# A message-passing kernel on one core: both edge tiles of a slot split into an fp32r pair, six block numbers in a word, three routing columns on GpSimd

## The reference, cut to what matters

```python
def _L0_gnn_ref(h, e, d2, ...):          # h = layernorm(x), d2 = edge weight
    hi, hj = h[e[0]], h[e[1]]
    msg = silu(concatenate((hi, hj, d2), -1) @ mW1 + mb1)
    msg = layer_norm(msg, ln_g, ln_b)
    msg = silu(msg @ mW2 + mb2)
    agg = segment_sum(msg, e[0], num_segments=3125)
    y = silu(concatenate((h, agg), -1) @ uW1 + ub1) @ uW2 + ub2
    return h + y
x = x + _L0_gnn_ref(layernorm(x), stack([src, dst]), edge_weight1, ...)
x = x + ffn(layernorm(x))   # top half of the nodes by a score goes through a gelu MLP
```

## Time and profile before

| | us |
|---|---|
| median of 3 runs | 2267.47 (2264.85 to 2274.99) |
| the profiled execution, whole | 2273.0 |
| its span | 2271.0 |
| TensorE busy | 1969.9 (87%) |
| VectorE busy | 1733.3 (76%) |
| ScalarE busy | 1314.6 (58%) |
| GpSimd busy | 1237.7 (54%) |

### The profile page before, as it was taken

How to read it: one execution, slowest core, us unless ns; L and a number is a source line. 1 busy time by engine, 2 the same in 40 slices (tenths; PEclk the granted TensorE clock), 3 DMA queues, 4 the chain that set the end, 5 groups by cost and what they waited for, 6 DMA issues and landing times. The chain is left out here.

```text
span 2271.0 us, 45335 instructions
## 1 busy us (share of the span) xinstructions
PE 1969.9 (87%) x11037; PEld 1679.3 (74%) x11038; DVE 1733.3 (76%) x4528; ACT 1314.6 (58%) x2595; POOL 1237.7 (54%) x1178
## 2 busy tenths in 40 slices
PE   3546674379999999999999999999999999799996
PEld 1324553267888888888888888888888888677775
DVE  5789999667778778778777787787787787436795
ACT  2322331256667777777776776777777677433331
POOL 7753222466666666666666666666666666503000
PEclk9987776589999999999999999999999999999998
DMA  3000000343333333333333333333333333010001
GB/s 123 0 1 21 26 26 18 102 136 124 87 87 95 92 87 93 97 87 94 96 93 86 94 96 87 91 95 93 90 94 95 88 92 92 1 40 2 27 1 57
DMA packets 107787, 165.05 MB, mean 73 GB/s; under 512 B 42141, under 2 KB 78330, under 8 KB 107485
## 3 DMA queue, kind: packets, MB, share of 16 engines
q0 software_dynamic: 42016, 111.40, 18.0%
q1 hardware_dynamic: 59822, 47.94, 6.8%
q10 hardware_dynamic: 5900, 5.08, 0.7%
HBM read 152.30 MB, written 11.65 MB: 72 GB/s over the span
## 5 line engine op out<-in xcount | busy, mean ns | idle before, releaser
L917 POOL DMA_INDIRECT g_rows<-b_table,idx_ring x792 | 763.3, 964 | 485.1 <-ACT act L967 277.8
L1048 PE MATMUL ps<-w2g,nT 128*128 128x256 f32 x3336 | 789.1, 379 | 0.0
L1048 PEld LDWEIGHTS ps<-w2g,nT 128*128 128x128 f32 x3336 | 601.5, 190 | 64.5
L956 ACT ACTIVATE normed<-act,shift,rstd_e 128x255 f32<-128x255 f32 x834 | 450.1, 590 | 16.1 <-DVE shift L1115 13.7
L1031 PE MATMUL psG<-msg,ohf 128*125 128x256 f32 x1668 | 429.9, 380 | 0.4 <-issue 0.4
L972 ACT ACTIVATE nT<-psM 128x512 f32<-128x512 f32 x417 | 248.7, 596 | 309.9 <-PE psM L1040 234.3
L1082 DVE TENSOR_TENSOR agg<-psG,agg 125x256 f32 x834 | 348.9, 418 | 88.2 <-PE psG L1031 30.9
L1022 PE MATMUL psH<-a_sb,ohT 128*128 x1668 | 348.1, 332 | 40.2 <-DVE ohT L1135 35.5
L1146 DVE TENSOR_TENSOR g_rows<-psH,g_rows 128x512 f32<-128x512 f32 x417 | 285.4, 684 | 67.2 <-issue 27.5
L1152 DVE BATCH_NORM_STATS2 stat_e<-act 128x6 f32<-128x256 f32 x834 | 311.0, 415 | 14.6 <-ACT act L967 14.6
L1022 PEld LDWEIGHTS psH<-a_sb,ohT 128*128 128x128 f32 x1668 | 260.1, 192 | 68.7 <-issue 48.4
(11 more groups left out here) (196 smaller groups left out, 1995.8 us busy)
## 6 DMA issues: line engine op xcount, KB each, us to landing
loc_rows<-loc_d SPq DMA_DIRECT2D x139, 187.5 KB
g_rows<-b_table,idx_ring POOLq DMA_INDIRECT x792
h_sb<-in_x SPq DMA_DIRECT2D x1, 3125.0 KB
b_table<-b_out SPq DMA_DIRECT2D x25, 125.0 KB
x_all<-in_x ACTq DMA_DIRECT2D x1, 3125.0 KB
out<-x_all SPq DMA_DIRECT2D x5, 625.0 KB
ohT<-ew_d SPq DMA_DIRECT2D x139, 9.0 KB
idx_ring<-rec SPq DMA_DIRECT2D x132, 3.0 KB
```

The costliest lines, as they stand in the source:

```text
L917: pool.indirect_dma_start(g_rows[:, j, n, :], None, b_table[:, :], bass.IndirectOffsetOnAxis(ap=which, axis=0)).then_inc(s_gather[j], 16)
L956: ins = nc.scalar.activation(normed[:, j % 2, n, 0:D - 1], act1[:, (j - 10) % RING, n, 0:D - 1], ACT.Identity, scale=rstd_e[:, g % 2, k:k ...
L1048: mm = pe.matmul(ps2[:, k, n, :], nT[:, k, n, q, :], w2g[:, q, :], start=(q == 0), stop=(q == 1))
```

## The change

- Each block's list is padded to a multiple of 256 edges, so both tiles of a pair belong to one block. PAIRS becomes 429, TILES 858.
- ScalarE writes the SiLU of ps twice: to high, rounded to fp32r, and, after act1, in full into ps2 (PSUM), over its input. VectorE makes low = ps2 - high (fp32r) as the last thing in its slot. TensorE sums ohf x high and ohf x low of both tiles into one region of psG, four fp32r matmuls; ohf is fp32r too.
- VectorE adds one region of psG to agg in each slot. Its block number comes from six_blocks, in which six numbers of five bits are packed (six VectorE instructions after routing): one word is loaded for six slots, shifted and masked in each.
- TensorE loads six block numbers for six slots.
- shift moves from the head of VectorE's slot to just ahead of g_rows; the later variance pieces move by one place each.
- Routing: VectorE writes 10 of the 13 mark columns, GpSimd the other three by tensor_scalar against iota_n, into four buffers that lie in f1 and f2. GpSimd makes those of steps 0 to 3 before the jump chain and those of step s+4 right after the scatter of step s. route(s) waits for them too.

```diff
-TILES = (EDGES + BLOCKS * (WIN - 1 + P - 1)) // P
-TILES += TILES % 2
-PAIRS = TILES // 2
+PAIRS = (EDGES + BLOCKS * (WIN - 1 + 2 * P - 1)) // (2 * P)
+TILES = 2 * PAIRS
+PG = -(-PAIRS // P)
...
+PCOLS = 3
+PRING = 4
...
+SIXES = (PAIRS - LAST % 6) // 6
+assert PAIRS % 3 == 0 and LAST % 6 == 3 and PAIRS % 6 == 3
...
+            or_ = sb("or_", [P, 2, COLS - PCOLS, P], BF16)
+            orp = [half[:, k * PCOLS * P // 2:(k + 1) * PCOLS * P // 2].bitcast(BF16).rearrange("p (t r) -> p t r", t=PCOLS)
+                   for half in (f1, f2) for k in range(PRING // 2)]
...
+                pool.tensor_scalar(tid[:, :], tid[:, :], 2.0, None, ALU.mult).then_inc(s_tid, 1)
...
+                def pool_columns(s):
+                    if s >= PRING:
+                        pool.wait_ge(s_win, s - PRING + 1)
+                    for k in range(PCOLS):
+                        c = s * COLS + COLS - PCOLS + k
+                        ins = pool.tensor_scalar(orp[s % PRING][:, k, :], iota_n[:, :], r_all[:, c:c + 1], None,
+                                                 ALU.is_equal)
+                    ins.then_inc(s_orp, 1)
+
+                pool.wait_ge(s_places, 1)
+                for s in range(PRING):
+                    pool_columns(s)
                 pool.wait_ge(s_upto, 1)
...
+                    if s + PRING < SUPERS:
+                        pool_columns(s + PRING)
...
+                    pe.wait_ge(s_orp, s + 1)
...
+                        marks = or_[:, s % 2, t, :] if t < COLS - PCOLS else orp[s % PRING][:, t - COLS + PCOLS, :]
+                        mm = pe.matmul(psK[:, s % 3, 0:PLANES * WIN], marks,
...
+                V.tensor_tensor(q_all[:, :], place[:, :], f2[:, :], ALU.subtract).then_inc(s_places, 1)
+                dve.wait_ge(s_places, 1)
...
+                link(V.tensor_scalar(rows_b[:, 0, :], upto[:, :, SUPERS - 1], WIN - 1 + P - 0.75, MAGIC_P, ALU.add, ALU.add))
...
+                    mine = slice(s * COLS, (s + 1) * COLS - PCOLS)
+                    V.tensor_tensor(or_[:, s % 2, :, :],
+                                    r_all[:, mine].unsqueeze(2).broadcast_to([P, COLS - PCOLS, P]),
+                                    iota_v.unsqueeze(1).broadcast_to([P, COLS - PCOLS, P]), ALU.is_equal)
...
+                dve.wait_ge(s_tbl, 16)
+                sixes = pair_block[0:1, 3:3 + 6 * SIXES].rearrange("a (m i) -> a m i", i=6)
+                link(V.tensor_copy(six_blocks[0:1, :], sixes[:, :, 5]))
+                for i in reversed(range(5)):
+                    link(V.scalar_tensor_tensor(out=six_blocks[0:1, :], in0=six_blocks[0:1, :], scalar=5,
+                                                in1=sixes[:, :, i], op0=ALU.logical_shift_left, op1=ALU.bitwise_or))
...
-            ohf = sb("ohf", [P, 2, 2, NB], F32)
+            ohf = sb("ohf", [P, 2, 2, NB], F32R)
             g_rows = sb("g_rows", [P, RING, 2, D], F32)
             act1 = sb("act1", [P, RING, 2, D], F32)
             normed = sb("normed", [P, 2, 2, D], F32)
             nT = sb("nT", [P, 2, 2, 2, P], F32)
-            msg = sb("msg", [P, 2, 2, D], F32)
+            high = sb("high", [P, 2, 2, D], F32R)
+            low = sb("low", [P, 2, 2, D], F32R)
...
-            psG = ctx.enter_context(nc.psum_tensor("psG", [P, 2, 2, D], F32))
+            psG = ctx.enter_context(nc.psum_tensor("psG", [P, 2, 2 * D], F32))
...
-                        nc.scalar.activation(msg[:, (j - 13) % 2, :, :], ps2[:, (j - 13) % 2, :, :], ACT.Silu).then_inc(s_msg, 1)
+                        nc.scalar.activation(high[:, (j - 13) % 2, :, :], ps2[:, (j - 13) % 2, :, :], ACT.Silu).then_inc(s_high, 1)
                     if has(t, 4):
                         act.wait_ge(s_hid, t - 3)
                         need(act, s_norm, t - 9)
                         nc.scalar.activation(act1[:, (j - 4) % RING, :, :], g_rows[:, (j - 4) % RING, :, :],
                                              ACT.Silu).then_inc(s_act1, 1)
+                    if has(t, 13):
+                        act.wait_ge(s_high, t - 12)
+                        nc.scalar.activation(ps2[:, (j - 13) % 2, :, :], ps2[:, (j - 13) % 2, :, :], ACT.Silu).then_inc(s_msg, 1)
...
-                regs = [pe.alloc_register(f"pe_block{n}") for n in range(2 * RING)]
+                regs = [pe.alloc_register(f"pe_block{n}") for n in range(RING)]
 
                 def prepare(d):
 
-                    lo = d * 2 * RING - 4
-                    n0, n1 = 0, 2 * RING
+                    lo = d * RING - 2
+                    n0, n1 = 0, RING
                     if isinstance(lo, int):
-                        n0, n1 = max(-lo, 0), min(n1, TILES - lo)
+                        n0, n1 = max(-lo, 0), min(n1, PAIRS - lo)
                     if n1 > n0:
-                        pe.reg_load(regs[n0:n1], tile_block[0:1, bass.ds(lo + n0, n1 - n0)])
+                        pe.reg_load(regs[n0:n1], pair_block[0:1, bass.ds(lo + n0, n1 - n0)])
...
+                        b = pe.snap(regs[j], min_val=0, max_val=BLOCKS - 1)
                         for n in range(2):
-                            b = pe.snap(regs[2 * j + n], min_val=0, max_val=BLOCKS - 1)
...
-                        pe.wait_ge(s_msg, t - 13)
+                        pe.wait_ge(s_low, t - 13)
                         pe.wait_ge(s_ohf, t - 13)
-                        need(pe, s_agg, 2 * t - 30)
+                        need(pe, s_agg, t - 15)
                         for n in range(2):
-                            mm = pe.matmul(psG[0:NB, k, n, :], ohf[:, k, n, :], msg[:, k, n, :], start=True, stop=True)
+                            pe.matmul(psG[0:NB, k, 0:D], ohf[:, k, n, :], high[:, k, n, :], start=(n == 0), stop=False)
+                            mm = pe.matmul(psG[0:NB, k, 0:D], ohf[:, k, n, :], low[:, k, n, :], start=False, stop=(n == 1))
...
-                        need(pe, s_msg, t - 13)
+                        need(pe, s_low, t - 13)
...
-                regs = [dve.alloc_register(f"dve_block{n}") for n in range(2 * RING)]
+                early = [dve.alloc_register(f"dve_block{n}") for n in range(3)]
+                packed = dve.alloc_register("dve_six")
+                block = dve.alloc_register("dve_block")
+                whole_from = -(-LAST // 6)
 
                 def prepare(d):
 
-                    lo = d * 2 * RING - 2 * LAST
-                    n0, n1 = 0, 2 * RING
-                    if isinstance(lo, int):
-                        n0, n1 = max(-lo, 0), min(n1, TILES - lo)
-                    if n1 > n0:
-                        dve.reg_load(regs[n0:n1], tile_block[0:1, bass.ds(lo + n0, n1 - n0)])
-
-                def add(t, j, n):
-                    b = dve.snap(regs[2 * j + n], min_val=0, max_val=BLOCKS - 1)
+                    if isinstance(d, int) and d < whole_from - 1:
+                        return
+                    if isinstance(d, int) and d == whole_from - 1:
+                        dve.reg_load(early, pair_block[0:1, 0:3])
+                    else:
+                        dve.reg_load([packed], six_blocks[0:1, bass.ds(d - whole_from, 1)])
+
+                def add(t, d, j):
+                    if isinstance(d, int) and d == whole_from - 1:
+                        b = dve.snap(early[j - 3], min_val=0, max_val=BLOCKS - 1)
+                    else:
+                        dve.reg_alu(block, packed, 5 * j, ALU.logical_shift_right)
+                        dve.reg_alu(block, block, 31, ALU.bitwise_and)
+                        b = dve.snap(block, min_val=0, max_val=BLOCKS - 1)
                     room = agg[:, bass.ds(b, 1), :].rearrange("p a n -> p (a n)")
-                    if n == 0:
-                        dve.wait_ge(s_sum, t - LAST + 1)
-                    need(dve, s_agg, 2 * (t - LAST) + n)
-                    V.tensor_tensor(room, psG[0:NB, (j - LAST) % 2, n, :], room, ALU.add).then_inc(s_agg, 1)
+                    dve.wait_ge(s_sum, t - LAST + 1)
+                    need(dve, s_agg, t - LAST)
+                    V.tensor_tensor(room, psG[0:NB, (j - LAST) % 2, 0:D], room, ALU.add).then_inc(s_agg, 1)
...
-                    shifts(t, d, j)
                     if has(t, LAST):
-                        add(t, j, 0)
+                        add(t, d, j)
                     variance(t, d, j, 1)
                     variance(t, d, j, 2)
                     variance(t, d, j, 3)
-                    if has(t, LAST):
-                        add(t, j, 1)
-                    variance(t, d, j, 4)
...
-                    variance(t, d, j, 5)
+                    variance(t, d, j, 4)
                     if has(t, 13):
                         V.tensor_tensor(ohf[:, (j - 13) % 2, :, :], nodes.unsqueeze(1).broadcast_to([P, 2, NB]),
                                         loc_e[:, bass.ds(2 * t - 26, 2)].unsqueeze(2).broadcast_to([P, 2, NB]),
                                         ALU.is_equal).then_inc(s_ohf, 1)
+                    variance(t, d, j, 5)
```

(32 more changed lines are left out.)

15 lines of the change are left out of this document (7 added, 8 removed).

## The result

Measured beside the kernel before, the changed kernel took 2338.44 us in the median of four runs (2334.52 to 2346.59) against 2268.81 (2264.85 to 2274.99): ratio 1.031, interval [1.027, 1.035]. The prediction, 2140 us (2105 to 2215) and faster, is wrong. The profiled execution took 2339.59 us, its span is 2337.8.

What follows compares the result with a forecast made beforehand. TensorE was taken to set the pace of the edge stage, two thirds of the run. 2273 us less 105 (edge stage) and 23 (routing) gives 2145, and 5.5 lower for the median 2140, range 2105 to 2215.

Steps and rivals of the forecast that it cites:

- (1): TensorE, psG: four fp32r passes take 0.48 us for 0.86; slot 3.12 us instead of 3.50, gain 0.38.
- (2): ScalarE: second SiLU, into PSUM, takes 0.48 us like the first (bounds nothing and 1.0); slot 2.93 us.
- (3): VectorE: one add less, low 0.59 us more, idle for number loads 2.6 to 0.4; slot 3.0 us taken.
- (4): End of VectorE's slot: low ready near 5.7 us, psG needs it at 6.7; one microsecond of cover.
- (5): TensorE loads six block numbers instead of twelve: nothing; without cover, at most 1.3 us in six slots.
- (8): Edge-stage stalls: today's 44 us stay, and 0.9 us more for each of 18 waits makes 60.
- Routing: VectorE's step 0.42 us shorter, 62 steps 26 us; 3 off for start and end; GpSimd's columns hidden; gain 23.
- Rival C: VectorE's sequencer: whole load, open shift and mask, wait for low make a 3.59 us slot; 2341 us; chance 0.04.
- A: Edge stage: ScalarE or VectorE becomes the bound at 3.2 to 3.3 us; 2196 us (2175 to 2217); chance 0.20.
- B: Routing: GpSimd becomes the bound, a column costing 0.8 us instead of 0.55; routing gains nothing, 2163 us; chance 0.08.
- D: TensorE: fp32r psG is no faster, slot stays 3.50 us; 2302 us; chance 0.03.
- E: VectorE's sequencer: load fixed and part of the rest, slot 3.35 to 3.42 us; 2240 to 2267 us; chance 0.05.

Runs made afterwards that it cites:

- on A: Chip of the first comparison: changed kernel 2338.44 us against 2268.81 for the kernel before.
- on C: Another chip of the same kind: changed kernel, unchanged, 2091.58 us against 2228.18 for the kernel before, ratio 0.939.
- high_twice: Changed kernel without the second SiLU and low, psG adding high twice; 2389.0 us, ratio 1.013 to the kernel before.
- on D: Chip of session 4: kernel before 2354.9 us; one_step_early 2355.6; changed kernel with psG in fp32 from one SiLU 2347.0.
- on B: Chip of session 1, on which the kernel before took 2356.5 us (2315 to 2407).
- routing_before: Changed kernel with all 13 columns of or_ on VectorE again; 2369.0 us, ratio 1.007 to the kernel before.
- the other three: Changed-kernel variants of that session: high_twice 2389.0 us; low made but not read by psG 2372.1; ohT's weight rows loaded only in the first body 2354.0.
- one_step_early: Changed kernel with only the first step's three columns ahead of GpSimd's jump chain, the other nine behind; 2355.6 us, ratio 1.002.
- after_again: Changed kernel, unchanged, beside the kernel before on another chip; 2091.6 us, ratio 0.939.
- before_here: Kernel before, unchanged, run for its trace; 2227.7 us.
- session 2: Follow-up session with before_here and three variants of the changed kernel; the kernel before took 2227.0 us.

## Why the prediction was wrong, step by step

**The pace was right.** (1) psG in four passes 0.11 to 0.12 us apart, slot 3.11 against 3.12. (2) The second SiLU is busy 0.59 us; catching up after a stall on A, normed starts at 875.91 and again at 878.88: 2.97 us, forecast 2.93. (3) VectorE's slots on C, which keep TensorE's pace on the whole, go down to 2.76 us from agg to agg (1046.13 to 1048.89), so 3.0 was too much; at the head of a body it idles 0.45 us, forecast 0.4 (wait on C, in 65 bodies):

```profile
DVE agg L1135 <- issue: 29.6, 65, 0.5
```

2.6 - 0.45 = 2.15 us for eleven loads less, 0.20 us each. The Trainium skill, "Runtime: NRT & Kernel Launch", section Instruction fetch mechanics, says some 200 ns for each register; it speaks of loads from HBM, these read a row of SBUF. The trace agrees. (4) low ends at 936.80 + 0.67 = 937.47 and psG starts at 938.03, so the cover is 0.6 us and not 1.0; on C that held, psG waited for low twice in all, for 1.1 us. (5), (6) Nothing, as forecast. (7) Twelve slots at 3.12.

**The step that failed is (8)**, the stalls: "44 us now, of a cause the trace doesn't name; I take it to stay", and 60 with the slower catching up. On A they were 249, on C 3. Too little time for ScalarE to catch up was not the reason: in high_twice its slot takes 2.46 us (nT at 604.51 and 606.97) instead of 2.97, and 290 us of stalls remained. What the 44 us stood for is TensorE's late signals: in the trace of the kernel before on A 88 of 1371 recorded updates are more than 1 us late, in that of the changed kernel 409 of 1295. In the kernel before this happened in a few clusters. One begins after a gather that started 2 us late (822.49 us): six follow each other from 825.01 on. GpSimd, with 8.87 us of work in the 10.5 us of three slots, soon returned to pairs. At 3.12 us a slot it has the same 8.87 us in 9.36, it falls into runs of four and six three times as often (90 against 29), and on A late signals came with nearly every such run. That the two belong together on such chips is shown by the counts, on A and, for two kernels beside each other, on D. Which causes which isn't shown, C shows that the runs alone do no harm, and why one chip's signals come late and another's don't stays open.

The stated 0.60 for a forecast with stalls of 25 to 90 us had no case for another chip: the kernel before was known from one, and on C the same kernel lands 13 us below the range.

**Routing** gained 13.5 us to the first ps (455.6 against 469.2), not 23; on B routing_before's first ps is 13 to 15 us behind the other three. Three readings. Steps: after dest there are 57 or_ in both traces of A, from 196.1 to 391.0 against 193.1 to 408.3: 56 steps take 20.2 us less, 0.36 each where 0.42 was forecast. Start: the twelve early columns took longer than their 6.6 us. From the trace on C, the first line VectorE, the second GpSimd:

```profile
160.01 3.39 DVE L752 TENSOR_TENSOR_SCAN agg<-agg 128x1550 f32<-128x1550 f32 x1
160.08 10.10 POOL L531 TENSOR_SCALAR x_all<-iota_n,x_all 128x128 bf16<-128x128 bf16 x12 [2.19 <-DVE x_all L746]
```

A column costs 0.59 us (three in 1.78), twelve 7.2; the other 2.9 are the scan's, which has two inputs in SBUF: in one_step_early the three columns beside it took 4.90 us, and the nine without it 5.29. The prediction was right that or_ isn't shut out (1.48 us beside columns, 10/13 of 1.88 being 1.45), but wrong that the page and the trace disagree there: "SBUF — State Buffer" of the Trainium skill, section Who interferes with whom, has VectorE instructions with two SBUF inputs contend with GpSimd, and or_ has one. The rule was needed one line earlier, at the scan, and there the trace agrees with it. dest is 3.0 us later than before (195.92 against 192.91 on A). End: GpSimd's step is one scatter of 1.05 and three columns, 3.05 us, hidden under 3.18 but too near to it to catch up, and it is further behind when VectorE is done. In after_again (last VectorE work of the steps, then the scatters):

```profile
391.74 1.46 DVE L783 TENSOR_TENSOR oqv<-psV,vals 128x1248 bf16<-128x1248 f32 x1
...
400.48 0.96 POOL L560 DMA_INDIRECT rec_d<-recw,dest  x1 [1.46 <-DMA rec_d<-recw,dest]
```

and in before_here:

```profile
409.15 1.46 DVE L752 TENSOR_TENSOR oqv<-psV,vals 128x1248 bf16<-128x1248 f32 x1
...
412.92 0.96 POOL L536 DMA_INDIRECT rec_d<-recw,dest  x1 [2.62 <-ACT recw L370]
```

The last scatter starts 8.7 us after the last oqv instead of 3.8: 5 us given back.

**The sum, without stalls:** from before_here (session 2) to after_again (C), two chips on which the kernel before takes the same time, the gain of 135.9 us (2225.0 - 2089.1 of span) is 1456.8 - 1337.1 = 119.7 in the edge stage, 12.6 ahead of it, 3.6 behind. The prediction's 416 x 3.50 - 428 x 3.12 + 23 is 144: the routing gave 10 us less than forecast, the stages behind the messages 4 us more.

**Rivals.** Rival C named nearly the time measured on A, 2341, but that is luck: it wanted a VectorE slot of 3.59 us, and the slot is 3.12. Rivals A, B, D and E did not happen either; that GpSimd's load would tell through the chip's late signals was none of them.

## What to carry to other kernels

A small stall of unnamed cause in the profile before is not a constant to be carried over: find out what it goes with (here, gathers that follow each other) and ask how often that will be so afterwards. This change, which took the slack of the engine that issues the gathers from 15% to 5%, was 6% faster on one chip and 3% slower on another; measure such a one on more than one chip before it is called either. Count the records of a trace, too: where a quarter of the semaphore updates of a stage is missing, recording itself is a suspect. And when work moves to GpSimd, look at what it reaches earlier or later at both ends of a stage.

## What the runs showed that was not expected

- The kernel before takes 2226 to 2229 us in the median on some chips and 2265 to 2407 on others, while the quiet slot is 3.50 us in both of its traces, one of each kind.
- On the latter, TensorE's signals, and no other engine's, reach ScalarE, VectorE and SyncE up to 6 us after the matmul that gives them, several within 0.2 us. The traces of these chips also lack 25 to 30% of the semaphore updates of the edge stage, the others 2% at most.
- An idle time of 2 us on TensorE was followed by a stretch of granted clock 0.60 in which ps took 3.58 us for 1.89.
- A VectorE tensor_scalar with one bfloat16 input in SBUF took 26.9 us for 0.34 beside ten GpSimd additions with two SBUF inputs: it was shut out until the last of them was done.
